# Feed-forward parameters prepared inside the second convolution, low halves on VectorE and row stores on GpSimd

## What is computed

```python
x = x + dwconv3x3(x, pos_w) + pos_b
n = layernorm(x, ln1)                      # over the 64 channels
q, k, v = n @ q_w + q_b, (n @ k_w + k_b) * SCALE, n @ v_w + v_b
lepe = dwconv5x5(v, lepe_w) + lepe_b       # per channel
# 8 heads of 8: softmax attention along each row, then along each column
a = attention_h(q, k, mask_h, attention_w(q, k, mask_w, v))
x = x + (a + lepe) @ out_w + out_b
y = layernorm(x, ln2)
x = x + gelu(y @ fc1_w + fc1_b) @ fc2_w + fc2_b    # 64 -> 256 -> 64
```

## Time and profile before

| What | Time |
|---|---|
| Three runs of the kernel before | 2121.85, 2123.58, 2132.22 us; median 2123.58 |
| The profiled execution | 2131.91 us |
| Its span, first to last instruction | 2130.0 us |
| Busy in the span: TensorE | 1847.2 us (87%) |
| VectorE, ScalarE, GpSimd | 1433.5, 1245.0, 1251.7 us |
| Mean granted clock of TensorE | 0.931 of 2.4 GHz |
| Second convolution, first to last instruction | from 1565.62; its convolutions start at 1592.87 |
| Feed-forward stage | from 1813.09 |
| Median from issue to landing: input of the convolution, row chunks of the feed-forward stage | 3.3 us, 2.5 us |

### The profile page before, as it was taken

One profiled execution on the slowest core, in us unless ns is written; L12 is line 12 of the kernel. 1 busy time (PEld: TensorE's weight loads), 2 busy tenths in 40 slices (PEclk: granted clock), 3 DMA queues, 4 the chain that ended last, 5 costly groups with the idle time before them and its releaser, 6 DMA issues. The chain is left out here.

```text
span 2130.0 us, 89180 instructions
## 1 busy us (share of the span) xinstructions
PE 1847.2 (87%) x34510; PEld 1542.2 (72%) x34510; DVE 1433.5 (67%) x2254; ACT 1245.0 (58%) x2107; POOL 1251.7 (59%) x1858
## 2 busy tenths in 40 slices
PE   5877425999999999999999999999959776599998
PEld 5877423888887888777877778878849776377776
DVE  3588965777776777766766667767635641688885
ACT  3677644555555555564555555555534656488887
POOL 6577856455554555544555545555544545499997
PEclk8988855999999999999999999999979987699999
DMA  9579656777877877788777787777756694455563
GB/s 141 99 184 226 179 175 152 172 175 179 180 167 170 181 176 172 163 184 186 180 173 178 179 183 173 183 171 181 160 106 129 149 223 149 104 137 138 135 139 83
DMA packets 666528, 346.82 MB, mean 163 GB/s; under 512 B 562462, under 2 KB 621598, under 8 KB 666254
## 3 DMA queue, kind: packets, MB, share of 16 engines
q1 hardware_dynamic: 636230, 311.54, 65.6%
q0 software_dynamic: 28864, 30.98, 5.3%
q10 hardware_dynamic: 1160, 0.13, 0.0%
HBM read 105.42 MB, written 102.76 MB: 98 GB/s over the span
## 5 line engine op out<-in xcount | busy, mean ns | idle before, releaser
L813 ACT ACTIVATE att_prob<-att_st_ps 128x448 f32<-128x448 f32 x896 | 486.3, 543 | 440.6 <-PE att_st_ps L720 440.5
L888 DVE TENSOR_REDUCE att_mm<-att_s_ps 128x8 bf16<-128x448 f32 x896 | 555.5, 621 | 266.9 <-PE att_s_ps L690 262.9
L733 PEld LDWEIGHTS att_pv_ps<-att_vx,att_prob 128*56 128x56 f32 x14336 | 560.6, 132 | 89.3 <-issue 5.1
L733 PE MATMUL att_pv_ps<-att_vx,att_prob 128*56 128x18 f32 x14336 | 513.5, 201 | 6.5 <-ACT att_prob L813 3.3
L582 POOL DMA_DIRECT2D att_mvt<-att_mneg x256 | 135.8, 535 | 560.3 <-ACT att_mneg L802 483.5
L690 PE MATMUL att_s_ps<-att_kx,att_q_unit 120*56 120x448 bf16 x1792 | 346.8, 360 | 9.5 <-DMA att_q_unit<-att_qk_hi 7.7
L715 PE MATMUL att_st_ps<-att_mvt,set_both 122*56 122x448 bf16 x1792 | 344.8, 357 | 11.4 <-DMA att_mvt<-att_mneg 10.4
L720 PE MATMUL att_st_ps<-att_qx,att_k_hi 128*56 128x448 bf16 x1792 | 343.5, 355 | 0.0
L720 PE MATMUL att_st_ps<-att_qx,att_k_lo 128*56 128x448 bf16 x1792 | 341.3, 352 | 0.0
L573 POOL DMA_DIRECT2D att_qx<-att_q_hilo x512 | 245.3, 487 | 2.0 <-issue 1.7
L796 ACT ACTIVATE att_qk_hi<-att_pj,set_bias 128x392 bf16<-128x392 f32 x256 | 150.2, 587 | 125.8 <-PE att_pj L648 125.5
(11 more groups left out here) (208 smaller groups left out, 3313.1 us busy)
## 6 DMA issues: line engine op xcount, KB each, us to landing
att_xt<-xn_chunks SPq DMA_DIRECT2D x128, 196.0 KB, 3.4
att_k_hi<-att_qk_hi SPq DMA_DIRECT2D x128, 196.0 KB, 3.5
att_k_lo<-att_qk_lo SPq DMA_DIRECT2D x128, 196.0 KB, 3.8
att_qx<-att_q_hilo POOLq DMA_DIRECT2D x512, 49.0 KB
pos_x<-in_x_dram SPq DMA_DIRECT2D x128, 105.0 KB
lepe_x<-v_scratch SPq DMA_DIRECT2D x128, 105.0 KB, 3.3
x_scratch<-pos_x SPq DMA_DIRECT2D x128, 98.0 KB
xn_chunks<-pos_xrt SPq DMA_DIRECT2D x16, 784.0 KB, 5.2
```

The lines of the kernel that those rows point to most:

```text
L733: ins = pe.matmul(pv_ps[v % 2][64 * h:64 * h + L, at:at + 18], prob[t % 4][:, 4 * h + a, :], vx[v][:, VW * j + 36 * a + 18 * h:VW * j + 36 ...
L813: act.activation(out, src, ACT.Exp).then_inc(exp_done, 1)
L888: dve.tensor_reduce(mm[v % 2][:, NH * j:NH * j + NH], s_ps[j % 2][:, 0:S8].rearrange("p (s k) -> p s k", k=L), AX.X, ALU.max).then_inc(max ...
```

## The change

Four things change in the second convolution and one in the feed-forward stage.

1. A class `MlpSetup` holds the feed-forward stage's parameters, its identity matrices and the steps that split them. The second convolution calls it: SP issues the 16 parameter DMAs in the step of image 0, VectorE clears in step 0 and splits in steps 6 to 12.
2. The low halves are made by VectorE, between its additions and copies; the ring `hl` has three tiles in place of four (SBUF room for the parameters).
3. VectorE's ring copies are plain `tensor_copy`.
4. The row stores are issued by GpSimd in step n for image n - 2, after `rezero(n)`.
5. The feed-forward stage starts with the loads of four row chunks and eight clearings; only the product for the bias `b1` is left of the preparations.

The first convolution keeps its order; its low halves go through the new function on GpSimd as before.

```diff
+class MlpSetup:
+    def parameters(self, sp):
+        par = self.par
+        for h in range(2):
+            p = slice(64 * h, 64 * h + 64)
+            sp.dma_start(self.wo_f[p, :], self.wo_d).then_inc(par, 16)
...
+        sp.wait_ge(self.bias_zero, 1)
+        for k in range(3):
+            sp.dma_start(self.bias_f[32 * k:32 * k + 1, 0, :], self.bo_d.unsqueeze(0)).then_inc(par, 16)
+        sp.dma_start(self.b2[:, :], self.bf2_d.partition_broadcast(128)).then_inc(par, 16)
...
+    def clear(self, dve):
+        dve.memset(self.bias_f[:, :, :].rearrange("p n c -> p (n c)"), 0.0).then_inc(self.bias_zero, 1)
+        self.done(dve.memset(self.ones_b[:, :], 1.0))
+        self.done(dve.memset(self.wo2[:, :], 0.0))
+        self.done(dve.memset(self.w12[:, :], 0.0))
+
+    def high(self, dve):
+        dve.wait_ge(self.par, 16 * 16)
+        self.done(dve.tensor_copy(self.wo1[:, :], self.wo_f[:, :]))
+        self.done(dve.tensor_scalar(self.w1_g[:, :], self.w1_f[:, :], self.g_c[:, 0:1], None, ALU.mult))
+        self.done(dve.tensor_copy(self.bias_p[0][:, :, :], self.bias_f[:, :, :]))
...
+    def weights(self, dve, n):
+        if n == 0:
+            self.clear(dve)
+        elif n == 6:
+            self.high(dve)
...
+        elif n == 12:
+            self.settled(dve)

 def conv_phase(...)
-        HL = 2 if pos else 4
+        HL = 2 if pos else 3
...
         def relay(eng, b, cg, done):
...
-            elif eng.engine == mybir.EngineType.DVE:
-                eng.tensor_tensor(dst, src, src, ALU.max).then_inc(done, 1)
             else:
                 eng.tensor_copy(dst, src).then_inc(done, 1)
+
+        def store_rows(eng, n):
+
+            eng.wait_ge(xr_sb, G * (n + 1))
+            eng.dma_start(xr_d[G * n:G * n + G].rearrange("g p t -> p g t"), xrt[n % 2][:, :, :]).then_inc(
+                xr_out[n % 2], 16)
+
+        def low(eng, n):
+
+            b, q = images[n]
+            t = hl[n % HL]
+            eng.wait_ge(hi_done, n + 1)
+            if n >= HL:
+                eng.wait_ge(tr_done, G * (n - HL + 1))
+            src = blocks(xc[n % 2][:, :, :]) if pos else image(b % 2, q)
+            eng.tensor_tensor(blocks(t[:, :, C:2 * C]), src, blocks(t[:, :, 0:C]),
+                              ALU.subtract).then_inc(lo_done, 1)
...
 SP, second convolution, step of image n
-                    if n >= LAG:
-                        store_t(n - LAG)
                     if b + 2 < NBATCH and q in (1, 2):
                         load(b + 2, 2 * q - 2)
                         load(b + 2, 2 * q - 1)
                     if n + 3 < B:
                         load_add(n + 3)
+                    if n == 0:
+                        mlp.parameters(sp)
...
 GpSimd, second convolution, step of image n
-                    lo(n)
                     rezero(n)
+                    if n >= 2:
+                        store_rows(pool, n - 2)
+            if not pos:
+                for n in (B - 2, B - 1):
+                    store_rows(pool, n)
...
 VectorE, second convolution, step of image n
+                    if q in (1, 2):
+                        low(dve, n + q - 1)
                     if q < 2:
                         add_attention(n + q)
-                    if n + 1 < B:
-                        b1, q1 = images[n + 1]
+                    b1, q1 = images[n + 1] if n + 1 < B else (NBATCH, 0)
+                    for cg in range(4):
                         if b1 + 1 < NBATCH:
-                            for cg in range(4):
-                                relay(dve, b1 + 1, 4 * q1 + cg, relaid_dve)
+                            relay(dve, b1 + 1, 4 * q1 + cg, relaid_dve)
+                        if q < 2 and cg == 1:
+                            add_attention(n + q + 1)
                     if q < 2:
-                        add_attention(n + q + 1)
+                        low(dve, n + q)
+                    mlp.weights(dve, n)

 SP, start of the feed-forward stage (the 16 parameter DMAs are gone)
-            sp.wait_ge(gaps, 1)
-            for v in range(NV - 1):
+            for v in range(4):
+                sp.dma_start(rt[v][:, :], rt_d[v]).then_inc(rt_in[v], 16)
+            sp.wait_ge(cleared, 4)
+            for v in range(4):
+                for r in range(2):
+                    sp.dma_start(x1[v][64 * r:64 * r + L, :, :], x1_v[v, r]).then_inc(x1_in[v], 16)
+            for v in range(4, NV - 1):
                 load(0, v)
...
 VectorE, start of the feed-forward stage (the splits are gone)
             for t in x1[0:4]:
-                done(dve.memset(t[32:64, :, :].rearrange("p j c -> p (j c)"), 0.0))
+                dve.memset(t[32:64, :, :].rearrange("p j c -> p (j c)"), 0.0).then_inc(cleared, 1)
             for t in (*o_ps[0:2], *y_ps):
-                done(dve.memset(t[:, :], 0.0))
...
+                dve.memset(t[:, :], 0.0).then_inc(cleared, 1)
+            dve.wait_ge(cleared, 8)
+            dve.sem_inc(ready, 1)
             dve.wait_ge(pre_pe, 1)
-            done(dve.tensor_tensor(b1[:, :], h_ps[0][:, 0:2], b1_in[:, :], ALU.add))
...
+            dve.tensor_tensor(b1[:, :], h_ps[0][:, 0:2], b1_in[:, :], ALU.add).then_inc(biased, 1)
             front(0, 0)
```

More of the change, by code:

```diff
@@ L1008, in conv_phase @@
         bsel = sb("bsel", [96, RB, WB], BF16)
[L1009 to L1010 removed]
+        ident = setup.ident if setup else mlp.ident
+        ident_b = mlp.ident_b if mlp else sb("ident_b", [128, 128], BF16)
         cv_ps = [al.ps(f"cv_ps{u}", [128, 512], F32) for u in range(4)]
@@ L1154, in _ @@
                         load_add(n + 3)
-            for n in range(B - LAG, B):
+                    if n == 0:
+                        mlp.parameters(sp)
+            for n in range(B - LAG, B if pos else 0):
                 store_t(n)
@@ L1221, in rezero @@
                     pool.memset(X[b % 2][0:64, q, :, 0, :], 0.0).then_inc(rezeroed, 1)
-            def lo(n):
-                b, q = images[n]
-                t = hl[n % HL]
-                pool.wait_ge(hi_done, n + 1)
-                if n >= HL:
-                    pool.wait_ge(tr_done, G * (n - HL + 1))
-                src = blocks(xc[n % 2][:, :, :]) if pos else image(b % 2, q)
-                pool.tensor_tensor(blocks(t[:, :, C:2 * C]), src, blocks(t[:, :, 0:C]),
-                                   ALU.subtract).then_inc(lo_done, 1)
             def ahead(n):
@@ L1246, in _ @@
                     if n:
-                        lo(n - 1)
+                        low(pool, n - 1)
                     pool.wait_ge(var_in, n + 1)
@@ L1254, in _ @@
                     if n == B - 1:
-                        lo(n)
+                        low(pool, n)
                 else:
-                    lo(n)
                     rezero(n)
+                    if n >= 2:
[3 more added lines that the diff above has]
+                    store_rows(pool, n)
         @block.tensor
@@ L1568, in mlp_phase @@
         y_ps = [al.ps(f"y_ps{u}", [128, 512], F32) for u in range(2)]
-        par, zeroed, unit, prep, pre_pe, ready, half_done = (
-            sem(n) for n in ("par", "zeroed", "unit", "prep", "pre_pe", "ready", "half_done"))
+        cleared, biased, pre_pe, ready, half_done = (
+            sem(n) for n in ("cleared", "biased", "pre_pe", "ready", "half_done"))
         rt_in = [sem(f"rt_in{u}") for u in range(4)] * 2
@@ L1574, in mlp_phase @@
         out_st = [sem(f"out_st{u}") for u in range(2)] * 4
-        rs_done, lo_done, bias_zero, gaps = (sem(n) for n in ("rs_done", "lo_done", "bias_zero", "gaps"))
+        rs_done, lo_done = sem("rs_done"), sem("lo_done")
         o_done, t_done, fc1_done, fc2_done = (sem(n) for n in ("o_done", "t_done", "fc1_done", "fc2_done"))
@@ L1785, in high @@
                 act.activation(hl[v][:, :, 0:C], xc[v][:, :, :], ACT.Copy).then_inc(hi_done, 1)
-            act.wait_ge(ready, 1)
             def turned(i, v):
@@ L1800, in gelu @@
                                    bias=b1[:, f:f + 1]).then_inc(gelu_done, 1)
+            act.wait_ge(biased, 1)
             for v in range(4):
@@ L1886, in _ @@
-            done(dve.tensor_copy(bias_p[1][:, :, :], bias_r[0][:, :, :]))
-            settled()
-            done(dve.tensor_tensor(bias_r[1][:, :, :], bias_r[0][:, :, :], bias_p[1][:, :, :], ALU.subtract))
-            settled()
-            done(dve.tensor_copy(bias_p[2][:, :, :], bias_r[1][:, :, :]))
-            settled()
-            for k in range(3):
-                done(dve.tensor_copy(bias_3[32 * k:32 * k + 32, :, :], bias_p[k][32 * k:32 * k + 32, :, :]))
-            dve.wait_ge(pre_pe, 1)
@@ L1895, in _ @@
-            done(dve.tensor_tensor(b1[:, :], h_ps[0][:, 0:2], b1_in[:, :], ALU.add))
-            dve.wait_ge(unit, 1)
-            done(dve.tensor_copy(ident_b[:, :], ident[:, :]))
-            settled()
-            dve.sem_inc(ready, 1)
+                dve.memset(t[:, :], 0.0).then_inc(cleared, 1)
+            dve.wait_ge(cleared, 8)
+            dve.sem_inc(ready, 1)
```

(10 more changed lines are left out.)

135 lines of the change are left out of this document (69 added, 66 removed).

## The result

The changed kernel takes 2104.76 us (median of 5 runs, 2103.56 to 2110.4) against 2125.37 for the kernel before: ratio 0.9898, 95% interval 0.9871 to 0.9925. The forecast was 2082 with a range from 2072 to 2101; of the 41.4 us it promised, 21 came. The profiled execution took 2110.4 us (span 2108.6) against 2131.9.

The account below looks back on a forecast made before the run. TensorE fills the feed-forward stage; the second convolution waits for input, GpSimd's low halves and row stores. Gains of 31.6 us there and 9.8 at the feed-forward start sum to 41.4: 2123.6 - 41.4 = 2082 us, range 2072 to 2101.

Parts of the forecast that it names:

- the time of the input loads: Second convolution: batch 2's input takes 28 us from first load to first copy, batch 3's 28 plus 1.4.
- free up to there: Second convolution's loop: GpSimd's row stores cost nothing if they land within 15.9 us of the copy.
- cold start: Second convolution, batch 2: after TensorE's wait for input the first group runs slower, adding 1.8 us.
- the feed-forward start: Start of the feed-forward stage: front(0, 0) begins at 1819.3 in place of 1829.1, a gain of 9.8 us.
- batch 1: Second convolution's four-image group in which TensorE turns only three: 36.2 us of TensorE work, never waiting for groups.
- the tail: Second convolution, from the end of batch 3's TensorE work to the stage end: 34.0 us in place of 31.1.
- Inputs in time: Rival, second convolution: loads move in 20 us or so, TensorE never stands; 8.6 us more gain, 2074; chance 0.15.
- Copies stay slow: Rival, second convolution: VectorE's ring copies still take 1.2 us each, giving 2089; chance 0.13.
- Stores late: Rival, GpSimd's row stores: landing in 12 us gives 2095, chance 0.11; beyond 15.9 us ScalarE waits, slower chance 0.04.
- that rival: Shared-port rule: VectorE's plain copies make GpSimd's stores some 2.5 us late, hidden in the loop; 2082, at worst 2087.

Follow-up runs that it names:

- the pad: Changed kernel with one unused tile of 32 bytes per partition behind the feed-forward parameters: 2105.4 us, ratio 0.9839.
- both moves of the parameters: Parameter loads issued behind batch 2's loads in the changed kernel, 2109.57 us; or by ScalarE, with 32 unused bytes and SP's row stores, 2090.36 us.

## Why the prediction was wrong

**The step that failed** is the time of the input loads: "Without the wait for the low half in the middle I take 28" for batch 2, and "28 us plus 1.4 for part of a second store" for batch 3. Both figures came from the kernel before, in which the tiles began 128 past a multiple of 256 and SP's queue kept all but one store out of the loads. With these two restored the loads take 28.5 and 28.8 us, batch 2's first copy comes 100.7 us behind the first load (forecast 99.4) and the stage starts at 213.2 (forecast 212.2). So the sum was right for a kernel that the diff does not make. Step by step, the changed kernel against the forecast: batch 2's loads begin 3.8 us later (75.2 behind the first load, forecast 71.4), take 5.6 us more, batch 3's take 6.4 more, and from batch 3's first copy to the stage it is 2.8 more, 18.6 in all. Two things that the diff does were not priced:

- Where tiles begin. No step of the prediction looked at what the moved allocations do to addresses. It cost 3 us ahead of everything (the first group at 1595.76 in place of 1592.87), some in each batch, 5.0 us of the stage with GpSimd's stores and 10.9 with SP's.
- The row stores' bytes. "GpSimd's store of image n need only be there when image n+2 is turned ...: free up to there" priced the wait for a store, rightly (3.0 us of waiting are left), and not what it takes from the loads beside it. That is 6.8 us of the stage in the changed kernel's place and 12.7 with the pad. The prediction itself said what should have warned: that batch 3's loads ran "at a DMA share near 1" (1.05 from 1700.6 to 1730.2; the earlier trace rows shows only the 0.80 of the whole stretch).

Each price depends on the other, so the 18.7 us (230.9 against 212.2) divide only together: 17.7 for both, 1.0 for the rest. Two small terms lie within these: the parameters took 9.7 us to issue, not 8.4 (1634.61 to 1644.3), and batch 3 had a cold start after 6.83 us of waiting (its work took 40.2 us, forecast 37.7), which the forecast gave only to batch 2, since it had the input there before TensorE was free.

**What held:** the feed-forward start (gain 9.3 of 9.8); low halves 2.02 us of 2.0, ring copies 0.71 of 0.68; TensorE full in the batches and waiting for nothing but input; batch 1 in 36.1 us of 36.2; the tail 34.4 of 34.0; no wait for row stores in the loop.

**The rivals.** "Inputs in time" was the wrong way in the changed kernel, and on 256 bytes with the parameters on ScalarE it is what happens: TensorE hardly stands. "Copies stay slow" did not happen; provoked, it cost 6.8 us of the stage against 6.6 forecast. "Stores late" did not happen: GpSimd's stores landed in 6.4 us (median in this stage) and 9.0 at most, where the case for it began at 15.9.

The rule on the port that VectorE and GpSimd share (the Trainium skill, SBUF — State Buffer, "SBUF: two separate sides") agrees with the changed kernel's trace in direction, not in size. Of the sixteen stores five are issued while VectorE makes plain ring copies, and GpSimd is busy 0.99 to 1.69 us with each of them; with the other eleven, two-input work of VectorE beside some of them, it is 0.75 to 0.77 us. One of the five, the copies beside it, and one of the eleven:

```profile
1693.28 1.01 POOL L1184 DMA_DIRECT2D r_rows<-lepe_xrt  x1 [1.54 <-ACT lepe_xrt L1476]
...
1711.74 0.75 POOL L1184 DMA_DIRECT2D r_rows<-lepe_xrt  x1 [4.94 <-ACT lepe_xrt L1476]
```

```profile
1693.27 1.33 DVE L1179 COPY lepe_xg<-lepe_x 128x480 f32<-128x480 f32 x2
```

That is 0.94 us of delay at the most, far from the 2.5 of that rival, and nothing waits for it: all five lie in the loop, where no engine waits for a store. (SP takes 372 to 440 ns to issue such a store in the kernel before.)

## What to carry to other kernels

When a diff allocates anything ahead of tiles that many small DMAs write, work out where those tiles begin, before and after; three tiles of 4 to 8 bytes in front took the input off a multiple of 256, and the way back was worth 16.5 us of the stage, more than most of the steps of this forecast. Before moving a store to an idle queue, ask which transfers it had been kept out of by standing behind them: here, with the DMA engines full, the order of SP's queue had kept the stores out of the loads' way, and "free" for the engine that issues was not free for the loads. And with the DMA engines full over two batches, what was gained ahead of the first came back as a wait at the second in both moves of the parameters off a multiple of 256.

## What the hardware did that was not expected

Packets of 256 bytes into SBUF took 17.7 ns each of a DMA engine's time (overlaps counted twice) when the tile began on a multiple of 256, 22.9 at 128 past one, 29.5 at 96 past, with the same loads at the same moment of the kernel; 64 loads were issued in 33.9, 37.7 and 43.5 us. The groups lie apart in every profile, but their sizes are rough: at 128 past, the kernel before alone gave 22.9 and 25.9 ns in two profiles.

The Trainium skill (DMA: Bandwidth & Descriptors, "How a descriptor splits into AXI transactions") says that a transaction has to start from a 256-byte boundary, so that a run that begins elsewhere costs extra beats. An estimate by its count: a 256-byte run costs 8 beats on the boundary, 8 + 4 = 12 at 128 past and 8 + 3 = 11 at 96 past. The first step agrees with the runs in direction (17.7 against 22.9 ns, 1.3 times and not 1.5); the second does not: 96 past is dearer than 128 past, not cheaper, so something else counts there too, and the page speaks of reads while it is the writes that are off the boundary here. No run here tells what.
